# The row of softmax maxima: turned by a matmul, or by VectorE in blocks of 32 with a trip through DRAM

## The reference

```python
ada = jax.nn.silu(c) @ W_ada + b_ada
shift_msa, scale_msa, gate_msa, shift_mlp, scale_mlp, gate_mlp = jnp.split(ada, 6, axis=-1)
h = _modulate(_layernorm(x), shift_msa, scale_msa)
x = x + gate_msa * _attention(h, W_qkv, b_qkv, W_proj, b_proj)
h = _modulate(_layernorm(x), shift_mlp, scale_mlp)
mlp = jax.nn.gelu(h @ W_fc1 + b_fc1, approximate=True) @ W_fc2 + b_fc2
x = x + gate_mlp * mlp
```

```python
scores = jnp.einsum('blhd,bmhd->bhlm', q * scale, k)
attn = jax.nn.softmax(scores, axis=-1)
o = jnp.einsum('bhlm,bmhd->blhd', attn, v).reshape(b, l, c)
```

## Time and profile before

| | |
|---|---|
| median of 3 runs | 3302.91 us |
| the profiled execution, its own time | 3299.94 us |
| its span | 3298.2 us |
| TensorE (PE) busy | 3279.3 us, 99% of the span |
| VectorE (DVE) busy | 2148.4 us, 65% |
| ScalarE (ACT) busy | 1695.5 us, 51% |
| GpSimd (POOL) busy | 359.6 us, 11% |
| granted TensorE clock, mean | 0.999 of full speed |
| DMA | 295.35 MB, mean 90 GB/s |

### The profile page before, as it was taken

The page is one execution under the profiler, slowest core; times in us unless marked ns, Lnnn a source line. Parts: engine busy times, 40 slices in busy tenths (PEclk is TensorE's granted clock), DMA queues, the critical chain, the costliest instruction groups (busy, mean ns, idle before and its releaser), DMA issues. The chain is left out here.

```text
span 3298.2 us, 52548 instructions
## 1 busy us (share of the span) xinstructions
PE 3279.3 (99%) x19303; PEld 2148.8 (65%) x19303; DVE 2148.4 (65%) x4008; ACT 1695.5 (51%) x3183; POOL 359.6 (11%) x284
## 2 busy tenths in 40 slices
PE   9999999999999999999999999999999999999999
PEld 7888744444444444444444444449989898989988
DVE  6445488888888888888888888857543433433332
ACT  4323377777777777777777777765521211211110
POOL 0000010111100000010000000026411010000000
PEclk9999999999999999999999999999999999999999
DMA  7554442333323232323232322318632122421211
GB/s 238 177 164 144 145 104 47 78 65 71 66 52 70 45 76 43 81 46 77 45 72 49 67 55 57 65 42 273 227 110 83 45 71 86 133 76 52 83 45 54
DMA packets 145167, 295.35 MB, mean 90 GB/s; under 512 B 22079, under 2 KB 45119, under 8 KB 137998
## 3 DMA queue, kind: packets, MB, share of 16 engines
q1 hardware_dynamic: 144910, 291.99, 32.9%
HBM read 192.95 MB, written 97.26 MB: 88 GB/s over the span
## 5 line engine op out<-in xcount | busy, mean ns | idle before, releaser
L1306 DVE TENSOR_REDUCE q_mx<-b_st 128x1 f32<-128x512 f32 x1512 | 989.6, 682 | 232.8 <-PE b_st L1234 229.2
L1377 ACT ACTIVATE b_pt<-b_st 128x512 f32<-128x512 f32 x2048 | 1055.5, 611 | 6.6 <-PE b_st L1254 6.5
L1266 PE MATMUL b_op<-b_pt,b_vs 128*37 128x512 f32 x4096 | 1008.4, 601 | 3.1 <-issue 1.6
L1370 ACT ACTIVATE b_early<-b_st 128x512 f32<-128x512 f32 x504 | 301.1, 597 | 476.7 <-PE b_st L1234 476.7
L1266 PEld LDWEIGHTS b_op<-b_pt,b_vs 128*37 128x37 f32 x4096 | 215.0, 113 | 368.4 <-issue 259.1
L1306 DVE TENSOR_REDUCE q_mx<-b_early 128x1 f32<-128x512 f32 x504 | 339.7, 674 | 1.2 <-ACT b_early L1370 1.2
L2121 PE MATMUL d_pm<-d_vh,d_ah 128*128 128x288 f32 x1152 | 339.4, 295 | 0.4 <-DVE d_al L2159 0.4
L2122 PE MATMUL d_pm<-d_vl,d_ah 128*128 128x288 f32 x1152 | 339.4, 295 | 0.0
L2123 PE MATMUL d_pm<-d_vh,d_al 128*128 128x288 f32 x1152 | 339.3, 295 | 0.0
L1440 POOL TENSOR_TENSOR w_oc<-b_oa,b_ob 37x512 f32<-37x512 f32 x127 | 161.4, 1271 | 1475.8 <-DVE b_ob L1344 1469.7
L1234 PEld LDWEIGHTS b_st<-q_hh,b_qa 36*128 36x128 f32 x1024 | 130.3, 184 | 225.8 <-DVE q_mx L1306 144.3
(11 more groups left out here) (412 smaller groups left out, 4769.6 us busy)
## 6 DMA issues: line engine op xcount, KB each, us to landing
qkh<-a_th SPq DMA_DIRECT2D x72, 256.0 KB, 2.0
qkl<-a_tl SPq DMA_DIRECT2D x72, 256.0 KB, 2.2
d_yi<-y SPq DMA_DIRECT2D x64, 288.0 KB, 3.0
n_oi<-hw SPq DMA_DIRECT2D x12, 1024.0 KB, 5.8
vd<-a_vx SPq DMA_DIRECT2D x8, 1184.0 KB, 6.3
b_vs<-vd SPq DMA_DIRECT2D x32, 296.0 KB, 7.6
a_x<-in_x SPq DMA_DIRECT2D x8, 1152.0 KB, 6.7
q_qs<-qkh SPq DMA_DIRECT2D x32, 288.0 KB
```

The source lines that it names most:

```text
L1266: ins = e.matmul(op[64 * a:64 * a + VW, :], vs[h % 2][:, j + 8 * a, :], pt[g % NP][:, a * 512:a * 512 + 512], start=j == 0, stop=j == 7)
L1306: e.tensor_reduce(mx[:, k // 2, col:col + 1], src, AX.X, ALU.max).then_inc(s_mx, 1)
L1370: e.activation(early[:, :], bank(slot)[:, :], ACT.Copy).then_inc(s_cp, 1)
L1377: e.activation(pt[g % NP][:, a * 512:a * 512 + 512], bank(k)[:, :], ACT.Exp, scale=SCALE).then_inc(s_p, 1)
```

## The change

The matmul that turned the maxima, its bank in the ring and its zero padding are gone. VectorE now does the whole of it in `row_max`, straight after the reduction: `nm` is 128 x 32 (columns 4 to 31 stay zero), `transpose` turns each 32 x 32 block of it on its own, so that row 32b + c of `nt` holds the maxima of queries 32b to 32b + 31 of column c; a copy makes `mh`, a subtraction `ml`, both 128 x 32. The four pieces of a row now lie on four partitions 32 apart. SP stores `mh` and `ml` whole to a DRAM tensor `md` (two DMAs of 16 KB), waits until both have landed, and then issues four DMAs that collect each row of 512 from 16 pieces of 128 bytes in `md`. There is one `nm`, one `nt`, one `mh` and one `ml`.

```diff
+    md = dram("md", [2, 128, 32])
...
-    nm = [A.sb(f"nm{i}", [128, VW]) for i in range(2)]
+    nm, nt = A.sb("nm", [128, 32]), A.sb("nt", [128, 32])
+    mh, ml = A.sb("mh", [128, 32], R), A.sb("ml", [128, 32], R)
...
-        s.slot = None if s.late is None else use("mh", s.late)
...
         def max_rows(p):
             h, u = divmod(p, 4)
             for j, m in enumerate((mh, ml)):
                 e.wait_ge(s_mh, 2 * p - 1 + j)
+                e.dma_start(md[j, :, :], m[:, :].bitcast(F)).then_inc(s_md, 16)
+            e.wait_ge(s_md, 32 * p)
+            for j in range(2):
                 for r in (ROWS - 2 + j, 64 + ROWS - 2 + j):
-                    e.dma_start(qb[h % NB][r:r + 1, u * 512:u * 512 + 512].bitcast(F), m[:, :].bitcast(F)).then_inc(
-                        s_m[h % NB], 16)
+                    e.dma_start(qb[h % NB][r:r + 1, u * 512:u * 512 + 512].bitcast(F),
+                                md[j, :, :].rearrange("(b c) t -> c b t", b=4)[0:4, :, :]).then_inc(s_m[h % NB], 16)
...
-        def max_rows(p, slot):
-            e.wait_ge(s_nm, p + 2)
-            bank_free(e, slot)
-            e.matmul(bank(slot)[0:VW, 0:128], nm[p % 2][:, :], ident[:, :], start=True, stop=True).then_inc(s_mt, 1)
...
             if s.now is not None:
                 products(2 * s.now)
-            if s.late is not None:
-                max_rows(s.late, s.slot)
             if s.now is not None:
                 products(2 * s.now + 1)
...
         def row_max(p):
+
+            e.wait_ge(s_nm, p)
+            if p > 1:
+                e.wait_ge(s_mx, 2 * (UQ * (p + 1) - THERE))
+                e.wait_ge(s_mt, p - 1)
+            q = p % 4 * 4
+            e.tensor_reduce(nm[:, 0:4], mx[:, q:q + 4, :], AX.X, ALU.max, negate=True).then_inc(s_nm, 1)
             e.wait_ge(s_nm, p + 1)
             if p > 1:
-                e.wait_ge(s_mx, 2 * (UQ * (p + 1) - THERE))
-            if p > 2:
-                e.wait_ge(s_mt, p - 2)
-            q = p % 4 * 4
-            e.tensor_reduce(nm[p % 2][:, 0:4], mx[:, q:q + 4, :], AX.X, ALU.max, negate=True).then_inc(s_nm, 1)
-
-        def max_rows(p, slot):
+                e.wait_ge(s_mh, 2 * p - 2)
+            e.transpose(nt[:, :], nm[:, :]).then_inc(s_mt, 1)
             e.wait_ge(s_mt, p)
             rows_there(e, p - 1)
-            src = bank(slot)[0:4, 0:128]
-            e.tensor_copy(mh[:, :], src).then_inc(s_mh, 1)
+            e.tensor_copy(mh[:, :], nt[:, :]).then_inc(s_mh, 1)
             e.wait_ge(s_mh, 2 * p - 1)
-            e.tensor_tensor(ml[:, :], src, mh[:, :].bitcast(F), ALU.subtract).then_inc(s_mh, 1)
+            e.tensor_tensor(ml[:, :], nt[:, :], mh[:, :].bitcast(F), ALU.subtract).then_inc(s_mh, 1)
```

More of the change, by code:

```diff
@@ L373, in program @@
                 lo0 = Q.sb("lo0", [128, 4, CH], R)
-                nm = Q.sb("nm", [128, 4])
-                mh = Q.sb("mh", [4, 128], R)
-                ml = Q.sb("ml", [4, 128], R)
                 qb0 = lo0[:, :, :].rearrange("p k t -> p (k t)")
@@ L380, in program @@
                     tile = phase_qkv(nc, Scope(nc, ctx, "a", top), ident, adaT, eps, bq, sc, qs0, ks0, qb0, hh0, lo0,
-                                     mx, nm, mh, ml, gd, xf, cond, W_ada, b_ada, W_qkv, b_qkv, qkh, qkl, vd)
+                                     mx, gd, xf, cond, W_ada, b_ada, W_qkv, b_qkv, qkh, qkl, vd)
                 E = Scope(nc, late, "e", top, "right")
@@ L396, in program @@
                     with ExitStack() as ctx:
-                        rest = phase_attention(nc, Scope(nc, ctx, "b", top), W, tile, ident, qs0, ks0, qb0, k1, mx, mh, ml,
-                                                gd, W_proj, b_proj, xf, qkh, qkl, vd, ot, sm)
+                        rest = phase_attention(nc, Scope(nc, ctx, "b", top), W, tile, ident, qs0, ks0, qb0, k1, mx,
+                                               gd, md, W_proj, b_proj, xf, qkh, qkl, vd, ot, sm)
                     N = Ahead(Scope(nc, late, "n", top, "right"), [hh0, ah0], [lo0, al0],
@@ L406, in program, with phase_qkv @@
                               b_fc2)
-def phase_qkv(nc, A, ident, adaT, eps, bq, sc, qs0, ks0, qb0, hh0, lo0, mx, nm, mh, ml, gd, xf, cond, W_ada,
+def phase_qkv(nc, A, ident, adaT, eps, bq, sc, qs0, ks0, qb0, hh0, lo0, mx, gd, xf, cond, W_ada,
               b_ada, W_qkv, b_qkv, qkh, qkl, vd):
@@ L433, in phase_qkv @@
     row0 = A.sb("row0", [66, 640])
+    nm, mh, ml = A.sb("nm", [128, 4]), A.sb("mh", [4, 128], R), A.sb("ml", [4, 128], R)
     wa = A.sb("wa", [128, KT, C])
@@ L1030, in phase_qkv, with phase_attention @@
     return LastTile(pm[(NCH * UN - 1) % 4][:, :], bq[:, NF - 1:NF], tf[0], th[0], tl[0], NCH * UN, s_mm, s_tf, s_tl, s_qo[0])
-def phase_attention(nc, A, W, tile, ident, qs0, ks0, qb0, k1, mx, mh, ml, gd, W_proj, b_proj, xf, qkh, qkl, vd,
+def phase_attention(nc, A, W, tile, ident, qs0, ks0, qb0, k1, mx, gd, md, W_proj, b_proj, xf, qkh, qkl, vd,
                     ot, sm):
@@ L1068, in phase_attention @@
     s_s, s_mx, s_nm, s_mt, s_mh = A.sem("s"), A.sem("mx"), A.sem("nm"), A.sem("mt"), A.sem("mh")
-    s_cp = A.sem("cp")
+    s_cp, s_md = A.sem("cp"), A.sem("md")
     s_st, s_p, s_pv, s_oa, s_oc = A.sem("st"), A.sem("p"), A.sem("pv"), A.sem("oa"), A.sem("oc")
@@ L1119, in bank_free @@
                 e.wait_ge(s_mx, n if n % 4 == 1 else n + 1)
-            elif kind == "mh":
-                e.wait_ge(s_mh, 2 * n)
             else:
@@ L1295, in score_max @@
             if p > 4:
-                e.wait_ge(s_nm, p - 2)
+                e.wait_ge(s_nm, p - 3)
             m, c = 2 * (n - THERE), k % 2
@@ L1332, in select @@
                 e.tensor_copy(cols[r:r + H, C:640], who[:, 512:C]).then_inc(W.s_sel, 1)
-        for t in nm:
-            e.memset(t[:, :], 0.0).then_inc(s_nm, 1)
+        e.memset(nm[:, :], 0.0).then_inc(s_nm, 1)
         row_max(1)
```

## The result

| | before | with the change |
|---|---|---|
| median of 5 runs | 3303.82 us | 3322.22 us |
| lowest and highest | 3302.2 and 3304.89 us | 3319.82 and 3332.61 us |
| the profiled execution, its own time | 3299.94 us | 3319.82 us |
| its span | 3298.2 us | 3318.1 us |
| PE busy | 3279.3 us | 3262.5 us |

The changed kernel takes 1.0065 of the time of before, with a 95% interval of 1.0054 to 1.0076: 18.4 us more. The forecast was 3311 us, slower, with a range of 3283 to 3345. So sign and range held, and the likeliest value was 11 us low. The profiled execution is the quickest of the five. Their scatter, 12.8 us against 2.7, already says that something in the changed kernel comes late by a varying amount.

What follows compares the result with a forecast made beforehand. PE was taken to set the pace in attention. The profiled 3299.94 us, less 24 for the matmul, plus 32 for late rows, gave 3308, or 3311 as a median; range 3283 to 3345 us.

Steps and rivals of the forecast that it cites:

- The matmul goes: Attention on PE: 127 turning matmuls removed, 0.19 us of pace each, 24 us less.
- DVE: Maxima on DVE: three new operations at 0.13 us each fit into its idle 0.72 us, cost 0.
- SP, first at T: A head's first trip on SP: stores, landing and four loads, so the head's loads begin 1.5 us earlier than before.
- T: The PE start of an attention step that has a head's loads in it; other times are counted from it.
- The block four steps on: A head's second block: its stores queue behind the head's loads and land about 25.7 us after the loads' step starts.
- Four loads: Second block's collecting loads on SP: last issued 1.27 us after the first, landing 1.8 us later.
- the dear end: Rival: loads issue near 0.6 us each or 128 B pieces are slow; 50 to 93 us lost, 3329 to 3372, chance 0.19.
- Late by 1.05 us: Second block's rows reach PE late by 1.05 us on average, over 31 heads 32 us more.
- The 2.0 us a DMA of the Trainium skill: Rule beside the rows: about 2.0 us fixed per DMA makes two landings 0.4 us later together, 12 us more, 3323.
- in time: Rival at the eighth step after a head's loads: rows arrive without real lateness, 3281 to 3294 us, chance 0.32.
- my chain: Second block's sequence from stores to landed loads, ending 28.9 us after the loads' step starts, 0.9 us late.
- The saving is not there: Rival: PE's 0.19 us are a disguised wait on DVE, which sets the pace; no gain, 3303 us, chance 0.05.

Runs made afterwards that it cites:

- no_trip: Changed kernel without the DRAM stores and wait; four small copies from a tile of zeros fill the rows instead: 3262.51 us, ratio 0.988.
- contiguous_four: Changed kernel with md laid out in row order, so each of the four loads reads 2 KB on end: 3272.86 us, ratio 0.9904.
- before_trip: Kernel before, matmul kept, with only the trip added: mh and ml stored to DRAM, awaited, each loaded twice: 3308.77 us, ratio 1.002.

## Why the prediction was right, and where it was off

The sum of the runs, each taken beside some 3303 us of the kernel before: the buffers' place -11 (3303.2 to 3292.2), the matmul -30 (3292.2 to 3262.5), the trip +60 (3262.5 to 3322.2), together +19; measured +18.4. The forecast had 0, -24 and +32.

- *The matmul goes*, "127 x 0.19 = 24 us": right in kind, 6 us short. Over all blocks the step that turned the maxima takes 3.67 us in the median before and 3.46 without the matmul, which makes 26 us. About half of the rest is in one step near the end of attention: the one from 2163.0 us takes 6.73 us before, partly at a halved clock (0.66 from 2165 to 2170 us), and 4.88 in no_trip. Why that one is shorter is not shown.
- *DVE*, "Cost 0, cover: DVE's slack": right, by 0.03 us. The three operations take 0.21, 0.18 and 0.19 us rather than 0.13, and the chain ends at 1232.63, where the next reduction starts at 1232.66.
- *SP, first at T*, "the head's loads begin at T + 4.3": T + 4.9. The landing took 1.5 us, not 1.8, which helps; the four collecting loads took 2.54 us, not 1.69, which hurts more.
- *The block four steps on*, "T + 25.7": SP is free at T + 25.4. Place and mechanism are as forecast, and the stores are through 20.5 us after the loads began, about 1 less than I had allowed.
- *Four loads*, "1.69 less its own 0.42": the term of the chain that was mis-sized. From the first start to the last it is 1.95 us (2.54 less 0.59), not 1.27: 0.65 us from start to start, beyond the 0.6 of the SBUF copies, which I had as the dear end, and not the 0.42 of sm. It counts twice, ahead of the loads and behind them. I had taken sm because it is small pieces from DRAM; but its transfers are 16 rows of 512 elements to 16 partitions, not 16 pieces of 128 bytes to one. contiguous_four shows what hangs on it: 49 us go by layout.
- *Late by 1.05 us*: by the starts of L1246, the 28 later heads with a wait are late by 35 us together, 1.14 us for each of 31; the forecast had 32 us. That close a hit is in part luck: the slow issue was nearly made up by a shorter landing and a shorter stay behind the loads.
- *Not in the sum at all*: what the broadcasts do to the first head (10 us for two steps, with its own halved clock), and the halved clock in five later heads (8 us together). With the 35 us that is 53 of the 57.5 us by which the profiled executions of the changed kernel and of no_trip differ. So the trip came out dearer than its 32 us by these two, for which the forecast had no term and gave no reason, and hardly by the lateness.
- *Not in the sum either*: the 11 us by buffers. I wrote that the rest of the program is not touched. Its instructions are not, its addresses are. This gain and the matmul's 6 us more go against the trip's 28 us more, and the total is nearer than its terms were; that is luck too.
- *The 2.0 us a DMA of the Trainium skill* (DMA: Bandwidth & Descriptors, section Anatomy of one DMA), by which the estimate was 3323: the total came out beside it, but not for that reason. The section gives its figure for DMAs that GpSimd issues; here SP does, and with nothing ahead both stores are through in 1.5 us (1218.97 to 1220.49), less than the rows of before had. No run shows a price for the read-modify-write that the same page of the Trainium skill, section Specifications, states for transfers under 512 bytes.
- *The chances*: the cases as listed add up to 0.32 faster, 0.23 same and 0.45 slower, where the prediction has 0.33, 0.20 and 0.47.

The rival "in time" lost: it wanted 0.6 us off my chain, and each group of four loads took 0.85 us more than I had for it. Its statement that little decides was right: before_trip and contiguous_four, with 1.4 us less at each of two places, fall on its side. "The saving is not there" is refuted by no_trip.

Left open: why buffers' addresses change PE's pace, why a DMA with 16 pieces takes 0.59 us to issue, and what decides whether the clock falls after a wait.

## What to carry to other kernels

A trip through DRAM is cheap or dear by what is ahead of it in the DMA engines and by how long its DMAs take to issue: cut the bulk loads by when each part is first wanted, and lay the small tensor out so that each load reads one stretch. A queue of its own need not bring a small transfer past a large one, and a wait in the issuing queue may be what keeps the large one back. Before a saving or a loss of 10 us is put down to an edit, compare at equal buffer addresses.

## What was not expected of the hardware

- Issue time on SP depends on the pattern: 0.59 us for 2 KB in 16 pieces of 128 bytes, 0.25 for 2 KB on end, 0.50 for the latter into two partitions; a store of 128 x 32 takes 0.34, the same store scattered into rows 0.51.
- A store of 16 KB behind 2.6 MB of loads lands 10.7 us after issue in their queue; from another engine's queue, with eight of the sixteen loads out by then, 9.6 us after issue; with nothing ahead, on SP, it is 1.5.
- A wait of 1.83 us in the midst of dense matmuls was followed by a granted clock of 0.50 for some 3 us, at a price of 1.7 us, one of 1.11 us by a like one; waits of 0.98 and of 1.79 us by none.
- Moving three small buffers changed how many matmuls PE gets through in 200 us from 1107 to 1119, at the same clock and the same busy time.
- A transpose of 128 x 32 in blocks of 32 takes VectorE 0.21 us, against 0.18 for a copy of that shape.
